# A delta-rule and expert layer on one core: the gate made in one ScalarE step, four loads from one queue, scatters a stage later

## What is computed

```
x = x + attn(layernorm(x)):
  q, k, v = conv4(hidden @ qkv_w)          # 8 heads of 128
  S = S * alpha_t;  S += k_t (v_t - k_t S) * beta_t;  o_t = q_t S
  o = o * rsqrt(mean(o^2) + eps) * norm_w
  o = o * (z * sigmoid(z)),   z = hidden @ z_w
  out = o @ out_w
x = x + moe(layernorm(x)):  8 experts, the 2 best of each token, relu MLP 128-512-128
```

## Time and profile before

| | us |
|---|---|
| median of 3 runs | 1395.7 (1393.5 to 1396.2) |
| the profiled execution, its own time | 1399.7 |
| its span, first to last instruction | 1397.9 |
| PE busy | 1199.9 (86%) |
| DVE busy | 1164.4 (83%) |
| ACT busy | 832.0 (60%) |
| POOL busy | 707.9 (51%) |

### The profile page before, as it was taken

One profiled execution on the slowest core, in us unless ns is written; L12 is line 12 of the kernel. 1 busy time (PEld: TensorE's weight loads), 2 busy tenths in 40 slices (PEclk: granted clock), 3 DMA queues, 4 the chain that ended last, 5 costly groups with the idle time before them and its releaser, 6 DMA issues.

```text
span 1397.9 us, 34191 instructions
## 1 busy us (share of the span) xinstructions
PE 1199.9 (86%) x12203; PEld 944.0 (68%) x12203; DVE 1164.4 (83%) x2531; ACT 832.0 (60%) x2536; POOL 707.9 (51%) x598
## 2 busy tenths in 40 slices
PE   0355999999999999999999999999999989479991
PEld 0233868686868687777777777777777767358881
DVE  6878898989898998989898989897989783578875
ACT  1252666666666666657566666756566655358884
POOL 3151727464555656473828292928192822235552
PEclk9997999999999999999999999999999998789996
DMA  6031212222221222131313141313121223432225
GB/s 208 0 98 32 73 35 73 47 69 62 54 63 53 62 54 64 52 68 48 84 34 91 28 98 25 103 28 88 30 85 43 73 55 98 104 96 78 76 65 181
DMA packets 163176, 97.10 MB, mean 69 GB/s; under 512 B 115623, under 2 KB 148269, under 8 KB 161988
## 3 DMA queue, kind: packets, MB, share of 16 engines
q1 hardware_dynamic: 124932, 82.25, 21.6%
q10 hardware_dynamic: 33536, 4.20, 2.1%
q0 software_dynamic: 4544, 8.47, 1.9%
HBM read 73.31 MB, written 24.61 MB: 70 GB/s over the span
## 4 chain that ended last, share of the span: by engine, by line
DVE 37%; PE 21%; POOL 17%; issue 10%; DMA 9%; SPq 3%; ACT 3%; POOLq 0%; DVEq 0%; ACTq 0%
DVE blkT L1060 9%; POOL kq L637 9%; DVE Y_sb L1056 9%; DMA blkN<-scr_n 4%; PE kx L1553 3%; POOL decay L629 3%; POOL rows_in L609 2%; DVE Gs L1204 2%; POOL kq L620 2%; DMA scr_n<-area 2%; PE rc L1717 2%; SPq L477 2%; DVE blkN L1047 1%; DVE area L1170 1%; DVE Y_sb L1043 1%
## 5 line engine op out<-in xcount | busy, mean ns | idle before, releaser
L637 POOL TENSOR_TENSOR kq<-tapA,area 128x256 f32<-128x256 f32 x256 | 252.0, 998 | 93.6 <-DVE area L1146 92.8
L758 ACT ACTIVATE area<-pj,taps 128x256 f32<-128x256 f32 x256 | 123.1, 481 | 142.7 <-PE pj L1567 136.5
L1056 DVE TENSOR_TENSOR Y_sb<-blkT,blkN 128x4 f32<-128x4 f32 (+18 forms) x304 | 169.5, 558 | 10.5
L609 POOL DMA_INDIRECT rows_in<-rowbuf,dest x64 | 64.6, 1009 | 202.1 <-DVE dest L1132 175.2
L1143 DVE SCALAR_TENSOR_TENSOR tapA<-pj,taps,tapA 128x256 f32<-128x256 f32 x256 | 122.2, 477 | 53.4 <-ACT tapA L758 51.6
L1553 PE MATMUL kx<-kq 128*128 128x128 f32 x1024 | 141.0, 285 | 20.0 <-ACT area L767 9.6
L1553 PEld LDWEIGHTS kx<-kq 128*128 128x128 f32 x1024 | 128.7, 197 | 38.4 <-issue 21.8
L620 POOL TENSOR_TENSOR kq<-kq,area 128x1024 f32<-128x1024 f32 x64 | 151.1, 2362 | 0.0
L1060 DVE TENSOR_REDUCE blkT<-Y_sb 128x2 f32<-128x4 f32 (+18 forms) x304 | 142.4, 469 | 5.2
L758 ACT ACTIVATE tapA<-pj,taps 128x256 f32<-128x256 f32 x256 | 123.0, 480 | 0.0
L1146 DVE SCALAR_TENSOR_TENSOR area<-pj,taps,area 128x256 f32<-128x256 f32 x256 | 121.4, 474 | 0.0
(11 more groups left out here) (307 smaller groups left out, 3613.2 us busy)
## 6 DMA issues: line engine op xcount, KB each, us to landing
area<-scr_alpha SPq DMA_DIRECT2D x32, 512.0 KB, 4.2
area<-scr_acum SPq DMA_DIRECT2D x32, 512.0 KB, 4.0
blkN<-scr_n SPq DMA_DIRECT2D x32, 256.0 KB, 4.4
area<-rows_in SPq DMA_DIRECT2D x39, 130.0 KB, 2.3
scr_n<-area SPq DMA_DIRECT2D x128, 32.0 KB, 1.6
area<-rows_out SPq DMA_DIRECT2D x4, 1024.0 KB, 8.1
rows_in<-rows_in SPq DMA_DIRECT2D x8, 260.0 KB, 3.8
kq<-in_x SPq DMA_DIRECT2D x4, 512.0 KB, 6.2
```

The costliest lines, as they stand in the source:

```text
L637: nc.gpsimd.tensor_tensor(dst[:, n % H, :], tapA[:, n % RING, :], tapB[:, n % RING, :], ALU.add).then_inc(conv_done, 1)
L758: ins = nc.scalar.activation(dst[:, n % RING, :], pj[n % 2][:, k:k + GT], ACT.Copy, scale=taps[:, t, k:k + 1])
L1056: ins = nc.vector.tensor_tensor(p4, bc(blkT[:, r0:, j:].rearrange("p r (o m) -> p r o m", o=1), [128, nr, w, wd]), bc(blkN[:, j:j + w, j:] ...
```

## The change

ScalarE applies Silu to z straight from PSUM into the tile zg; it now waits for the last reader of the tile (g_ready) itself, and its end frees the bank. VectorE's step zg has no instructions any more; `ow` loses the factors for the half and for WSCALE. SyncE issues all four loads of T64 in `ti`; `tj` is gone. `sc` stands in the middle of the stage, behind `last.15`, and scatters there the rows of the group before the one that is routed (r - 1); the last two groups are scattered behind the stages. `ka.0` stands ahead of `last.0` instead of behind `first.3`.

```diff
 ORDER:
-  ... proj.3 m.0.0 last.0 taps.3 rdiag.0 me.1.0 v.0.1 first.2 proj.4 first.3 ka.0 last.1 ...
+  ... proj.3 m.0.0 ka.0 last.0 taps.3 rdiag.0 me.1.0 v.0.1 first.2 proj.4 first.3 last.1 ...
-  ... g.1.0 last.15 kd.1.0 inv.13 ... st.1.1 xs.1 tj sc
+  ... g.1.0 last.15 sc kd.1.0 inv.13 ... st.1.1 xs.1
 SyncE, step ti:
-                        for b in (0, 1):
+                        for b in range(NB):
                             r = slice(BLK * b, BLK * b + BLK)
-                            sp.dma_start(T64.rearrange("p g h c -> p (g h) c")[r, :, r], inverses[b]).then_inc(t_in, 16)
+                            sp.dma_start(T64.rearrange("p g h c -> p (g h) c")[r, :, r if b < 2 else slice(0, BLK)],
+                                         inverses[b]).then_inc(t_in, 16)
 GpSimd:
-                    if r is not None:
+                    if step == "sc" and r is not None and r > 0:
+                        route("sc", r - 1, par)
+                    elif step != "sc" and r is not None:
                         route(step, r, par)
...
             stages(NG - 1, None, 0)
+            route("sc", NG - 2, 1)
 ScalarE:
-                    elif step == "tj":
-                        act.wait_ge(t_out, a * 32 + 32)
-                        for b in (2, 3):
-                            act.dma_start(T64.rearrange("p g h c -> p (g h) c")[BLK * b:BLK * b + BLK, :, 0:BLK], inverses[b]).then_inc(t_in, 16)
...
                         c, u = arg
+                        if g is not None:
+                            act.wait_ge(g_ready, halves(g, c, u))
                         act.wait_ge(z_mm, halves(a, c, u))
-                        nc.scalar.activation(zg[:, c, HU * u:HU * u + HU, :], heads(pj[u]), ACT.Tanh,
-                                             scale=0.5 / WSCALE).then_inc(z_tanh, 1)
+                        nc.scalar.activation(zg[:, c, HU * u:HU * u + HU, :], heads(pj[u]), ACT.Silu,
+                                             scale=1.0 / WSCALE).then_inc(zg_ready, 1)
 VectorE:
-            nc.vector.tensor_scalar(ow[:, :, :], ow[:, :, :], nw[:, 0:1], 0.5 / WSCALE / VSCALE, ALU.mult,
+            nc.vector.tensor_scalar(ow[:, :, :], ow[:, :, :], nw[:, 0:1], 1.0 / VSCALE, ALU.mult,
...
-                    elif step == "zg":
-
-                        c, u = arg
-                        dve.wait_ge(z_tanh, halves(a, c, u))
-                        nc.vector.scalar_tensor_tensor(out=half(zg, c, u), in0=half(zg, c, u), scalar=1.0,
-                                                       in1=heads(pj[u]), op0=ALU.add, op1=ALU.mult).then_inc(zg_ready, 1)
```

More of the change, by code:

```diff
@@ L197, in preln_delta_moe_kernel @@
         (diag_ready, decay_done, kk_ready, n_ready, ktr_ready, kd_ready, scale_ready, kq_ready, at_ready,
[L198 removed]
+         ka_ready, aq_ready, z_mm, zg_ready) = sems(
             "diag_ready decay_done kk_ready n_ready ktr_ready kd_ready scale_ready kq_ready at_ready ka_ready "
[L200 removed]
+            "aq_ready z_mm zg_ready")
         (blk_in, inv_step, inv_done, t_out, t_in, rdiag) = sems("blk_in inv_step inv_done t_out t_in rdiag")
@@ L249, in preln_delta_moe_kernel @@
         ORDER = """
[L250 to L263, removed]
@@ L264, in preln_delta_moe_kernel @@
-            st.1.1 xs.1 tj sc
-            """
+        proj.0 proj.1 taps.0 taps.1 diag.0 first.0 v.0.0 proj.2 m.1.0 taps.2 al.0 first.1 proj.3 m.0.0 ka.0
+        last.0 taps.3 rdiag.0 me.1.0 v.0.1 first.2 proj.4 first.3 last.1 me.0.0 m.1.1 taps.4 proj.5 me.1.1
+        ks.0.0 m.0.1 taps.5 scan.0 first.4 m.1.2 proj.6 me.0.1 rdiag.1 ks.0.1 last.2 last.3 first.5 me.1.2
+        proj.7 m.0.2 m.1.3 al.1 taps.6 diag.1 first.6 taps.7 last.4 proj.8 first.7 kk.0.0 me.0.2 me.1.3 m.0.3
+        last.5 proj.9 last.6 xl.0 rhs.0.0 me.0.3 last.7 sp.0 scan.1 nm.0.0 taps.8 kk.0.1 u.0.0 taps.9 aq.0
@@ new lines, in preln_delta_moe_kernel @@
+        nm.0.1 kk.1.0 first.8 last.8 nm.1.0 kk.1.1 nm.1.1 proj.10 ue.0.0 rhs.0.1 taps.10 o.0.0 first.9 proj.11
+        first.10 proj.12 u.0.1 taps.11 first.11 taps.12 last.9 sd.0.0 proj.13 ktr.0.0 ue.0.1 first.12 xl.1
+        aq.1 last.10 no.0 no.1 sq.0.0 proj.14 taps.13 last.11 st.0.0 ac.0 sd.0.1 taps.14 g.0.0 o.0.1 first.13
+        ka.1 st.0.1 sq.0.1 proj.15 last.12 v.1.0 sm v.1.1 scale.0 bi ks.1.0 kd.0.0 first.14 inv.0 taps.15
+        ks.1.1 last.13 rhs.1.0 inv.1 inv.2 last.14 inv.3 inv.4 first.15 rhs.1.1 u.1.0 inv.5 kq.0.0 u.1.1
@@ new lines, in preln_delta_moe_kernel @@
+        ue.1.0 g.0.1 inv.6 ue.1.1 o.1.0 o.1.1 ktr.0.1 sq.1.0 inv.7 s2 ac.1 sd.1.0 sp.1 sq.1.1 kd.0.1 inv.8
+        scale.1 inv.9 inv.10 at.0.0 inv.11 ktr.1.0 inv.12 g.1.0 last.15 sc kd.1.0 inv.13 rms.0 inv.14 sd.1.1
+        ktr.1.1 kd.1.1 rms.1 gn.0.0 kq.0.1 gn.0.1 gt.0.0 inv.15 at.0.1 z.0.0 inv.16 gt.0.1 gte.0.0 nr g.1.1 xt
+        inv.17 gte.0.1 z.0.1 zt.0.0 xe lg out.0 gn.1.0 zt.0.1 inv.18 rk gn.1.1 gt.1.0 inv.19 gt.1.1 x2.0
+        inv.20 gte.1.0 inv.21 kq.1.0 gte.1.1 pf out.1 zg.0.0 z.1.0 tp zt.1.0 zg.0.1 ps st.1.0 z.1.1 zt.1.1
@@ L266, in preln_delta_moe_kernel @@
+        zg.1.0 zg.1.1 xs.0 x2.1 to at.1.0 kq.1.1 at.1.1 ti st.1.1 xs.1
+        """
         STEPS = [(name, *map(int, arg)) for name, *arg in (word.split(".") for word in ORDER.split())]
@@ L705, in _ @@
                 nc.scalar.activation(wv_hi[:, k, :], wv_taps[k], ACT.Copy, scale=-VSCALE).then_inc(s_vhi, 1)
-            for t in (z_tanh, kd_ready, rhs_ready, u_ready, sq_done, gn_ready, gt_ready):
+            for t in (zg_ready, kd_ready, rhs_ready, u_ready, sq_done, gn_ready, gt_ready):
                 act.sem_inc(t, HALVES)
@@ L1015, in _ @@
             dve.wait_ge(s_zero, 1)
-            for t in (n_ready, at_ready, zg_ready, S_ready, g_ready):
+            for t in (n_ready, at_ready, S_ready, g_ready):
                 dve.sem_inc(t, HALVES)
```

## The result

The changed kernel takes 1448.9 us (median; 1447.5 to 1451.2) against 1396.0 us beside it (1393.5 to 1398.0). The ratio is 1.038, with a 95% interval of 1.036 to 1.041: 53 us slower. The forecast was 1430 us, slower, with a range from 1402 to 1446. The direction was right, the size 19 us short, and the result lies 3 us outside the range.

What follows compares the result with a forecast made beforehand. Each turn is bound by T64's trip, then nearly full TensorE, then VectorE in the inverse. Terms 1.3 + 1.6 + 17.2 + 18.5 - 4 = +34.6 us; against the 1395.7 us median, 1430 us, range 1402 to 1446.

Steps and rivals of the forecast that it cites:

- Term 1: In the inverse's trip to DRAM and back: taking zg (2.6 us a stage) off VectorE is hidden by the trip; 0.
- Rival D: Middle stretch: fourth T64 load 0.9 us late (1445), or TensorE's clock drops after longer waiting (1444); chance 0.06.
- A: The main forecast, all terms summed: 1430 us, from 1408 to 1450 with the locks' ends; chance 0.64.
- Term 2: ScalarE: Silu for Tanh costs 0 off the path; two more table loads cost 0 to 2.6 us, taken as 1.3.
- Term 3: SyncE issues all four T64 loads: later start mostly paid by absent scatters, 0.1 us a turn, +1.6 us.
- Term 4: Scatters moved a stage later, beside the inverse: they don't lengthen VectorE's instructions there; 0.
- rival E: Inverse: the scatters hold VectorE too, each up to 0.97 us, +54 us on top, 1484; chance 0.03.
- Terms 5 and 6: End of the inverse: GpSimd's early diag.0 and ka.0 each hold a VectorE product beside them; +17.2 and +18.5 us.
- term 6: End of the inverse: ka.0 at its new place holds VectorE's 128x450 product, +1.1 us in 14 turns; +18.5 us in sum.
- term 5: End of the inverse: diag.0, no longer held back, holds VectorE's 128x351 product 1.32 us in 13 turns; +17.2 us.
- Term 7: Middle stretch without scatters, diag.0 and ka.0 at its head: 0.3 us shorter in 13 turns, -4 us.
- rival C: Middle stretch: GpSimd was the bound, so faster; 0.86 us a turn without a lock, 1385; chance 0.14.

Runs made afterwards that it cites:

- b_gate: Kernel before the change, with only the gate's part (Silu on ScalarE with its g_ready wait, zg off VectorE, output weights' scale): 1418.9 us, ratio 1.016.
- b_gate_fill: b_gate plus five stand-in products of 128x512 (results unused) on TensorE just before proj.2: 1403.2 us, ratio 1.005.
- b_silu_zg: Kernel before the change, with Silu for Tanh on ScalarE, but VectorE keeping a zg instruction of the same shape that passes the value through: ratio 1.001.
- a_no_gate: Changed kernel without the gate's part (Tanh and zg as before; loads, scatters and ka.0 as changed): 1426.8 us, ratio 1.021.
- b_scat: Kernel before the change, with only GpSimd's part (scatters a stage later, ka.0 ahead of last.0): 1419.7 us, ratio 1.017.
- a_ka_late: Changed kernel with ka.0 back at its old place behind first.3, diag.0 still beside the inverse: 1431.1 us, ratio 1.024.
- b_scat_hold: b_scat with GpSimd's diag.0 (and ka.0 behind it) waiting for the end of the running inverse: 1385.7 us, ratio 0.992.

## Why the prediction was right in direction and short in size

*Term 1, zg off VectorE, "I take 0": this step failed.* VectorE's 2.6 us were hidden, as said (its wait for T64 rose from 6.9 to 41.3 us). But the step asked only what VectorE does with the time. The instruction also releases banks that TensorE waits for, and with it gone TensorE came early and stood idle. The part costs 22 us alone (b_gate) and 24 in the change, where the prediction had 0. b_gate_fill against b_gate puts 15 us of that down to the idle time and the clock behind it; b_silu_zg excludes Silu.

*Rival D, the clock, was named and mis-weighed.* It gave +1.5 us a turn in nine turns, on top of A's sum, and so 1444; the trace has 1.6 us in ten turns, one of them twice that. A's locks and D's falls both happened: 1430 plus 13 to 16 us is 1443 to 1446, most of the way to 1449. The prediction had the link from VectorE's 2.6 us to TensorE's longer wait, but only here, with a chance of 0.06 that it shared with a late fourth load; term 1 stayed at 0, and nothing of D went into the sum.

*Term 2, Silu and tables, 1.3:* right. b_silu_zg gives +2 (-2 to +5), and both new table loads took 1.28 us, as the earlier trace rows:

```profile
L786 ACT ACT_TABLE_LOAD x1 | 1.3, 1283 | 0.0
L905 ACT ACT_TABLE_LOAD x1 | 1.3, 1283 | 0.0
```

The 5.3 us that the prediction named beside its own 1.3 do not show: the load of L905 starts at 1344.42, 0.02 us after the instruction before it has ended, and the next one starts at 1345.72, 0.02 us after the load.

*Term 3, the loads, 1.6:* 5 alone, inside its ends, and 6 in a_no_gate against b_scat. In the change itself the transpose came 3.74 us after the first load's issue, against 4.06 before; without scatters beside the loads that is sooner, but b_scat, with the loads in two queues, had 3.72 and a VectorE that never waited for them. So the prediction was too favourable in letting the later scatters pay for the later start.

*Term 4, the scatters beside the inverse, 0:* right, rival E is out. They took 1.04 instead of 1.01 us, and no product beside them grew by more than 0.03 us. The Trainium skill (SBUF — State Buffer, "Who interferes with whom") would have had a product with two SBUF inputs contend with a GpSimd instruction that reads SBUF. For diag.0 and ka.0 the rows agree; for the scatters they show no hold.

*Terms 5 and 6, the two locks, 17.2 + 18.5 = 35.7:* right in place, cause and size. The inverse grew by 33.8 us in 15 turns, and the held products are longer by 34.5 us in all. The split holds roughly: a_ka_late takes 14 us from the inverse (and 20 from the time, with fewer falls among them) for term 6, which leaves 19 for term 5.

*Term 7, the middle stretch, -4: mis-sized.* In b_scat it is 0.57 us a turn shorter (8.6 us, some 3 of them the two falls that it lacks), and the trip 0.34 (5 us), because T64 lands sooner without scatters beside it. That is the gain of rival C, real but not enough: its "1385" for the gain without a lock is what b_scat_hold measured, 1385.7. In the change most of it was lost, to the loads (27.9 us for the middle stretch also in a_no_gate, without a fall) and to the clock. The first scan took 3.2 to 4.3 us in 13 of the 15 turns before and takes 2.28 in 12 of 15 now, as the prediction said. None of that shows in the time beyond the gain named here, since TensorE fills the middle stretch.

So the errors ran both ways. Predicted and measured by part: the gate 1.3 and 22 us, the loads 1.6 and 5, GpSimd's part 35.7 - 4 = 31.7 and 23. That the sum came within 19 us is in part luck: the loss at the gate was put 21 us too low, and the loss at GpSimd 9 us too high. Together the parts have 34.6 and 50; the 3 us between 50 and the change's 53 are of the size of the intervals.

Two things more. Of the signs of being wrong one came: four trips of 8.4 to 8.7 us, beyond the 8.2 given for D. They are the four turns with a late store (last section), not a late fourth load. And the ends of A, 1408 to 1450, do not follow from the ends of its terms: both locks at their least give 1430 - 35.7 = 1394, at their most 1430 + 7.5 + 19.5 = 1457.

## What to carry to other kernels

When an instruction is taken off an engine that waits anyway, look at whom it released: the engine behind it may run ahead and wait too, and behind TensorE's wait its granted clock fell here, for 1.6 us each time. When an engine is relieved, ask what its next instruction will now run beside. Here one semaphore wait, which kept GpSimd's product out of the inverse, turned the relief of GpSimd from 23 us of loss into 11 of gain. And a rival that can happen on top of the forecast belongs into the sum, weighed by its chance, not beside it.

## What was not expected of the hardware

**A store was late where instructions were fetched beside it.** From the issue of blkT's store to that of T64's first load it takes 3.7 us in every turn of the kernel before, of b_scat and of b_silu_zg. In every kernel without zg it takes 4.4 to 5.3 us in 4 to 6 of 16 turns. Two turns of b_gate, from SyncE's queue:

```profile
675.41 0.55 SPq L490 DMA_DIRECT2D scr_t<-blkT  x1
680.01 0.85 SPq L496 DMA_DIRECT2D T<-scr_t  x2
...
747.26 0.55 SPq L490 DMA_DIRECT2D scr_t<-blkT  x1
750.92 0.85 SPq L496 DMA_DIRECT2D T<-scr_t  x2
```

The DMA view of 676.40 to 676.90 in the same kernel has, beside the store's queue, a transfer of instructions:

```profile
q8 instruction: 1, 0.02, 13.7%
```

Over the stores of all turns of the fourteen kernels: in every turn with 4.4 us or more a transfer of instructions begins 1.1 to 3.0 us after the store's issue. Where none begins in that time it is 3.6 to 4.0 us. The reverse does not hold throughout: in five turns with such a transfer at 2.6 to 2.7 us it took only 3.9 to 4.2. That is some 1.3 us in a third of the turns, about 6 us in a run, all of it in the trip. Why the transfers fall there only in the kernels without zg is not shown, and no run moved a transfer alone, so this stays a coincidence in the traces.

**Equal waits, unequal clocks.** Every fall in the middle stretch of the changed kernel follows TensorE's wait for T64. But VectorE's wait there was 2.17 us in a turn with a fall (the second shown above) and 2.17 us in one without. TensorE's own gap just ahead of the merge tells more and not all: 1.37 to 2.71 us in the ten turns with a fall, 0.47 to 1.51 us in the five without. What decides between turns with like gaps stays open; the runs show only that filling the wait takes nearly all the falls away.
